# Another order of the work in each step of three narrow cross attentions

## The chip, the cores and the metric

The kernel is one program on 1 core of a Trainium2 chip. The metric is the device time of one execution in microseconds (us); the median of three executions of the kernel before is 3112.84 us.

## What is computed

Four layers of a perceiver: each adds a cross attention to `x` (32 samples, 64 queries, width 256), then a mixing stage, then a feed-forward stage. The change touches the cross attentions of layers 1, 2 and 3. They have one formula, cut here to what matters:

```
q = ln(x @ Wq + bq)                      16 heads of 16, normed per head
k = ln(y_main @ Wk + bk)                 112 context rows of a sample
v = y_main @ Wv + bv
k_dca, v_dca = the same from y_dca       the other 16 context rows
ctx = attn(q, k, v) + attn(q, k_dca, v_dca)
x = x + ctx @ Wo + bo
```

The two softmaxes of a head, over 112 and over 16 context rows, are separate, so each has its own maximum and its own sum.

## The kernel before

The function `cross_attention_narrow` (called three times, for L1, L2 and L3) writes one program for each engine by hand, with semaphores between them. Its main part is a loop over steps `n`, from -1 to 34. In a step the samples stand at different places of a pipeline:

- **score** (L1540, TensorE): the scores of sample n+1 into the buffer `p_s`. There is one such buffer, so it waits for `shifted`, sample n's subtraction on VectorE.
- **maximum** (L1772), **subtraction** (L1782), **row sums** (L1790) and **reciprocal** (L1793) on VectorE; the sums are those of sample n-1. ScalarE's **exponential** (L1701) is sample n's. GpSimd multiplies with the reciprocals (L1856, semaphore `normed`) and then spreads the queries of sample n+2 (L1849, `q_spread`, for which that sample's score waits).
- **values** (L1551, TensorE): sample n-2, into the bank `p_v`; ScalarE's two **value copies** (L1710, L1712, `v_copied`) move it to `vx`.
- **turn** (L1561, TensorE): 8 transposes of sample n-2's probabilities into `p_t`; ScalarE's two **probability copies** (L1728, `turned_read`) move them out.
- **mix** (L1574, TensorE): probabilities by values of sample n-3; ScalarE's **u copy** (L1718, `mixed_read`) moves the result out.
- **output product** (L1581, TensorE), in even steps from 4 on, for two samples; VectorE's **x addition** (L1798, `added`), in odd steps from 5 on, reads it. The mix two samples on waits for that addition, because both use the bank `p_y`.

Beside this nine **units** (three of queries, six of keys, 512 columns each) are normed for later samples. A unit takes three steps, and from step 4 on the kinds of step repeat by threes:

- **kind A** (steps 4, 7, ... 22): TensorE's **unit product** (L1499 for queries, L1503 for keys) into `p_t`, ScalarE's **bias** (L1652, `biased`) and **squares** (L1667, `squared`). The turn of this step waits for the bias, because it uses the same `p_t`.
- **kind B** (steps 5, 8, ... 23): TensorE's **tally** (L1517), which adds the squares up in the bank `p_v`, and ScalarE's **inverse** (L1684 and L1687 or L1691).
- **kind C** (steps 6, 9, ... 24): TensorE's **widening** (L1527) into `p_t`, VectorE's **unit multiplication** (L1766, `scaled`), for which this step's turn waits. GpSimd's addition L1841 follows.
- steps 25 to 34 have no unit; from step 31 on there is no score either.

The order of the work is written out in the `step` function of each engine, and every engine takes its instructions in that order. TensorE's order before, in one step:

```
score(n+1); unit product or widening; values(n-2); mix(n-3);
tally, after a wait for v_copied of values(n-2);
turn(n-2), in kinds A and C after biased or scaled; output product
```

ScalarE's: exponential, bias, value copies, u copy, inverse, probability copies, squares. VectorE's: maximum, unit multiplication, subtraction, row sums, reciprocal, x addition.

Of the kernel before, what the change touches and what calls it, by code (L numbers as in the profile page):

```python
# [1341 lines left out]
def cross_attention_narrow(k, layer):  # L1342
# [9 lines left out]
    with ExitStack() as ctx:  # L1352
# [83 lines left out]
        def within(n, lo, hi):  # L1436
            return lo <= n < hi
# [14 lines left out]
        def _(pe):  # L1452
# [91 lines left out]
            def values(n):  # L1544
                if n >= 1:
                    pe.wait_ge(sem["v_copied"], n)
                else:
                    pe.wait_ge(ln.sem["rstd"], 1)
                    pe.wait_ge(s_o, 32)
                pe.wait_ge(sem["logged"], tallied_before(n + 2))  # L1550
                pe.matmul(p_v[:, :], k.ctxT[:, ts(n, S2)], wv[:, :, :].rearrange("p n f -> p (n f)"), start=True, stop=True, skip_group_check=True).then_inc(sem["valued"], 1)  # L1551

            def turn(n):
# [30 lines left out]
            def step(n):  # L1584
                if -1 <= n < B - 1:
                    score(n + 1)
                units = at_step(n)
                for i, part in units:
                    if part == 0:
                        turned_before(n)  # L1590
                        project(i)
                    elif part == 2:
                        turned_before(n)
                        widen(i)
                if within(n, 2, B + 2):
                    values(n - 2)
                if within(n, 3, B + 3):
                    mix(n - 3)
                for i, part in units:
                    if part == 1:  # L1600
                        if n >= 2:
                            pe.wait_ge(sem["v_copied"], n - 1)
                        else:
                            pe.wait_ge(ln.sem["rstd"], 1)
                        tally(i)
                if within(n, 2, B + 2):
                    for i, part in units:
                        if part == 0:
                            pe.wait_ge(sem["biased"], i + 1)
                        elif part == 2:  # L1610
                            pe.wait_ge(sem["scaled"], i + 1)
                    turn(n - 2)
                if n >= 4 and n % 2 == 0:
                    project_out((n - 4) // 2)

            ln.means(pe)
            keep_warm(pe, k, p_tw[:, 0, :], 1)
# [27 lines left out]
        def _(act):  # L1645
# [48 lines left out]
            def own(n, rows):  # L1694
                return vx[rows, n % 2, :, :, :].rearrange("p o (r j) (s d) -> p (o r) (j s) d", j=2, s=2)[:, :, 0:4:3, :]

            def step(n):
                units = at_step(n)
                if within(n, 0, B):
                    act.wait_ge(sem["shifted"], n + 1)  # L1700
                    act.activation(prob[:, n % 4, :, :, :], prob[:, n % 4, :, :, :], ACT.Exp, scale=0.25).then_inc(sem["exped"], 1)  # L1701
                for i, part in units:
                    if part == 0:
                        add_bias(i)
                if within(n, 2, B + 2):
                    m = n - 2
                    act.wait_ge(sem["valued"], m + 1)
                    if m >= 2:
                        act.wait_ge(sem["mixed"], m - 1)
                    act.copy(own(m, slice(0, P)), p_v[:, 0:D].rearrange("p (g j d) -> p g j d", j=2, d=HD)).then_inc(sem["v_main"], 1)  # L1710
                    act.wait_ge(sem["v_main"], m + 1)
                    act.copy(own(m, slice(0, DCA)), p_v[0:DCA, D:2 * D].rearrange("p (g j d) -> p g j d", j=2, d=HD)).then_inc(sem["v_copied"], 1)  # L1712
                if within(n, 3, B + 3):
                    m = n - 3
                    act.wait_ge(sem["mixed"], m + 1)
                    if m >= 4:
                        act.wait_ge(sem["out_proj"], m // 2 - 1)
                    act.copy(us[:, m // 2 % 2, :, ts(m % 2, S)], p_o).then_inc(sem["mixed_read"], 1)  # L1718
                for i, part in units:
                    if part == 1:  # L1720
                        inverse(i)
                if within(n, 2, B + 2):
                    m = n - 2
                    for o in range(H2):
                        act.wait_ge(sem["turned"], 2 * m + o + 1)
                        if m >= 1:
                            act.wait_ge(sem["mixed"], m)
                        act.copy(probT[:, o, :, :, :].rearrange("p r j t -> p (r j t)"), p_t[:, o, :, :].rearrange("p r q -> p (r q)")).then_inc(sem["turned_read"], 1)  # L1728
                for i, part in units:
                    if part == 0:  # L1730
                        squares(i)
# [28 lines left out]
        @block.vector  # L1760
        def _(v):
            def multiply(i):
                kind, c = UNITS[i]
                dst = q if kind == QN else kk
                v.wait_ge(sem["widened"], i + 1)
                v.tensor_tensor(dst[:, :, ts(c, CH)], biased[:, i % 2, :, :], front(i)[:, :, :], ALU.mult).then_inc(sem["scaled"], 1)  # L1766

            def step(n):
                if within(n, 0, B):
                    v.wait_ge(sem["scored"], n + 1)  # L1770
                    for m, (s0, s1) in enumerate(SEG):
                        mx = v.tensor_reduce(nmax[:, n % 2, m, :, :], p_s[:, :, :, s0:s1], AX, ALU.max, negate=True)  # L1772
                    mx.then_inc(sem["maxed"], 1)
                for i, part in at_step(n - 1):
                    if part == 2:
                        multiply(i)
                if within(n, 0, B):
                    v.wait_ge(sem["maxed"], n + 1)
                    if n >= 4:
                        v.wait_ge(sem["turned"], 2 * n - 6)  # L1780
                    for m, (s0, s1) in enumerate(SEG):
                        sub = v.tensor_tensor(prob[:, n % 4, :, :, s0:s1], p_s[:, :, :, s0:s1], bcast(nmax[:, n % 2, m, :, :], 3, s1 - s0), ALU.add)  # L1782
                    sub.then_inc(sem["shifted"], 1)
                if n < H2:
                    out_bias_of(n)
                if within(n, 1, B + 1):
                    m = n - 1
                    v.wait_ge(sem["exped"], n)
                    for seg, (s0, s1) in enumerate(SEG):
                        total = v.tensor_reduce(rsum[:, 0, m % 4, seg, :, :], prob[:, m % 4, :, :, s0:s1], AX, ALU.add)  # L1790
                    total.then_inc(sem["summed"], 1)
                    v.wait_ge(sem["summed"], n)
                    v.reciprocal(rsum[:, 1, m % 4, :, :, :], rsum[:, 0, m % 4, :, :, :]).then_inc(sem["recip"], 1)  # L1793
                if n >= 5 and n % 2 == 1:
                    t = (n - 5) // 2
                    v.wait_ge(sem["out_proj"], t + 1)
                    v.wait_ge(sem["biased_x"], 2)
                    v.tensor_tensor(k.x[:, :, ts(t, P)], k.x[:, :, ts(t, P)], p_y, ALU.add).then_inc(sem["added"], 1)  # L1798

            def add_bias(i):  # L1800
                kind, c = UNITS[i]
                v.wait_ge(sem["projected"], i + 1)
                v.wait_ge(sem["copied"], 2)
                for o in range(H2):
                    to, of = (ap.rearrange("p (b s) -> p b s", s=S2) for ap in (biased[:, i % 2, o, :], front(i)[:, o, :]))
                    for (m, to), (_, of) in zip(columns(kind, to), columns(kind, of)):
                        j = v.tensor_scalar(to, of, bc[:, m, o:o + 1], None, ALU.add)
                j.then_inc(sem["biased"], 1)

            def out_bias_of(o):  # L1810
                v.wait_ge(sem["out_bias"], 2)
                v.wait_ge(ln.sem["centred"], NCH)
                v.tensor_scalar(k.x[:, o, :], k.x[:, o, :], out_bias[:, 1, o:o + 1], None, ALU.add).then_inc(sem["biased_x"], 1)

            for c in range(NCH):
                ln.centre(v, c)
            add_bias(0)
            ln.scale(v, 0)
            ln.scale(v, 1)
            multiply(0)  # L1820
            ln.scale(v, 2)
            ln.scale(v, 3)
            multiply(1)
            multiply(2)
            for n in range(B + 4):
                step(n)
# [1835 lines left out]
```

## Time and profile before

| | |
|---|---|
| median of 3 executions (3112.57 to 3114.63) | 3112.84 us |
| span of the profiled execution | 3107.8 us |
| median less that span (what lies around the span) | 5.0 us |
| instructions in the span | 49980 |
| TensorE matmul busy | 2746.9 us, 88% |
| VectorE busy | 1863.8 us, 60% |
| ScalarE busy | 1414.8 us, 45% |
| GpSimd busy | 993.6 us, 32% |

The own time of the profiled execution is its span and what lies around it; the runs list times without naming the profiled one, so the median stands for it. Most of the span belongs to stages that the change does not touch. The main loops of the three stages lie at about 905 to 1089, 1587 to 1771 and 2107 to 2290 us of the span. A busy TensorE is not one at its peak, since matmuls overlap and their ends are modelled; distances between the starts of groups say more. A number in square brackets behind an instruction is the time that its engine sat idle before it, with what ended that time.

### The profile page before, as it was taken

The page shows a single profiled execution, that of the slowest core. Times are in us where ns is not written, and L with a number is a line of the kernel's source. Part 1 is how long each engine was busy: PE and PEld are TensorE (multiplying, and loading weights), DVE is VectorE, ACT ScalarE, POOL GpSimd, SP SyncE. Part 2 cuts the span into 40 slices and gives each one's busy share as a digit, 9 for nine tenths or more (in the row PEclk, how much of TensorE's full clock was granted, in tenths as well). Part 3 has the DMA queues.
Part 4 walks back from the last instruction along what each step waited for, and adds up shares of the span by engine and source line. Part 5 has one row for each costly group of instructions (what it writes and reads, how often), then busy time and mean ns, then how long its engine had stood idle before and what let it go on. Part 6 is the DMA issues. An engine that isn't in the chain of part 4 may idle for free. (4 is left out here: it accounts for less than half of the span.)

```text
span 3107.8 us, 49980 instructions
## 1 busy us (share of the span) xinstructions
PE 2746.9 (88%) x18724; PEld 1708.9 (55%) x18724; DVE 1863.8 (60%) x2492; ACT 1414.8 (46%) x2714; POOL 993.6 (32%) x836
## 2 busy tenths in 40 slices
PE   8999997999989988899989875668989798999899
PEld 5989863466556647433346532225644455554687
DVE  3555546322258737444468678767865799996433
ACT  4333345122147646322257554445767666653123
POOL 0111100133225512000035400005520799992462
PEclk9999998999999999999999988889999999999999
DMA  4000003311110000200000000000000212113124
GB/s 159 1 0 0 0 7 112 114 47 46 55 50 2 2 22 2 85 1 0 2 21 2 15 0 0 0 22 2 2 30 18 77 69 80 68 58 112 57 87 150
DMA packets 73446, 122.61 MB, mean 39 GB/s; under 512 B 11616, under 2 KB 54240, under 8 KB 72736
## 3 DMA queue, kind: packets, MB, share of 16 engines
q1 hardware_dynamic: 64320, 95.48, 9.2%
q0 software_dynamic: 8928, 24.39, 2.5%
q8 instruction: 137, 2.24, 0.3%
q14 instruction: 61, 0.50, 0.1%
HBM read 101.10 MB, written 18.74 MB: 39 GB/s over the span
## 5 line engine op out<-in xcount | busy, mean ns | idle before, releaser
L3398 POOL TENSOR_TENSOR h<-ssm_u,ss_bc 128x1024 f32<-128x1024 f32 x88 | 205.6, 2354 | 0.0
L3361 ACT ACTIVATE ssm_p_h<-ss_delta,ss_decay 128x256 f32<-128x256 f32 x352 | 146.6, 463 | 123.9 <-DVE ctxT L3435 82.9
L3308 PE MATMUL ssm_p_y<-ctxT,ident 128*128 128x512 f32 x412 | 187.8, 596 | 0.0
L650 POOL TENSOR_TENSOR xw_prob<-xw_prob,xw_rsum 128x512 f32<-128x512 f32 x64 | 65.8, 1039 | 355.2 <-DVE xw_rsum L631 355.2
L3430 DVE TENSOR_TENSOR_SCAN ssm_p_h<-ssm_p_h,h 128x1024 f32<-128x1024 f32 x64 | 145.8, 2279 | 8.7 <-ACT ssm_p_h L3361 6.8
L3388 POOL TENSOR_TENSOR ctxT<-ctxT,ss_bc 128x1024 f32<-128x1024 f32 x50 | 117.4, 2355 | 19.3 <-DVE ctxT L3428 19.3
L500 PEld LDWEIGHTS xw_p_q<-h,xw_m_h 128*128 128x128 f32 x1024 | 116.8, 192 | 8.9 <-issue 8.9
L509 PEld LDWEIGHTS xw_p_q<-xw_u,xw_vo_h 128*128 128x128 f32 x1024 | 115.8, 192 | 10.7 <-ACT xw_u L580 10.2
L3308 PEld LDWEIGHTS ssm_p_y<-ctxT,ident 128*128 128x128 f32 x412 | 76.6, 192 | 79.5 <-issue 78.3
L509 PE MATMUL xw_p_q<-xw_u,xw_vo_h 128*128 128x128 f32 x1024 | 118.2, 276 | 0.0
L500 PE MATMUL xw_p_q<-h,xw_m_h 128*128 (+1 forms) x1024 | 117.0, 275 | 1.3 <-PEq L60 1.3
L3292 PE MATMUL ssm_p_h<-ssm_b_diagonal,ssm_uT 128*128 128x128 f32 x640 | 82.9, 284 | 39.9 <-DVE ctxT L3435 19.5
L2432 ACT ACTIVATE lmm_hidden<-lmm_p_h,vecs 128x512 f32<-128x512 f32 x64 | 43.5, 687 | 156.0 <-PE lmm_p_h L2392 108.1
L3292 PEld LDWEIGHTS ssm_p_h<-ssm_b_diagonal,ssm_uT 128*128 128x128 f32 x640 | 77.7, 197 | 63.8 <-issue 55.2
L1196 DVE TENSOR_TENSOR L0f_hidden<-L0f_silu,L0b_p_u 128x512 f32<-128x512 f32 x39 | 26.8, 688 | 125.2 <-PE L0b_p_u L1131 125.2
L621 DVE TENSOR_TENSOR xw_prob<-xw_p_s,xw_mask_bias 128x512 f32<-128x512 f32 x64 | 44.0, 687 | 91.7 <-PE xw_p_s L518 91.7
L2461 DVE TENSOR_TENSOR lmm_hidden<-lmm_hidden,lm_weights 128x512 f32<-128x512 f32 x64 | 44.1, 689 | 89.5 <-ACT lmm_hidden L2432 89.5
L1830 POOL MEMSET L3x_vx<- 128x1024 f32 x1 | 1.0, 952 | 302.2 <-POOLq L60 302.2
L1856 POOL TENSOR_TENSOR L1x_prob<-L1x_prob,L1x_rsum 128x896 f32<-128x896 f32 x64 | 65.3, 1042 | 73.5 <-DVE L1x_rsum L1793 73.5
L1856 POOL TENSOR_TENSOR L2x_prob<-L2x_prob,L2x_rsum 128x896 f32<-128x896 f32 x64 | 65.3, 1042 | 73.5 <-DVE L2x_rsum L1793 73.5
L1856 POOL TENSOR_TENSOR L3x_prob<-L3x_prob,L3x_rsum 128x896 f32<-128x896 f32 x64 | 65.3, 1042 | 72.3 <-DVE L3x_rsum L1793 72.3
L1105 POOL DMA_INDIRECT L0f_rows_out<-L0b_y,L0f_row_of x39 | 38.5, 986 | 146.7 <-DVE L0b_y L1204 146.7
(865 smaller groups left out, 7146.6 us busy)
## 6 DMA issues: line engine op xcount, KB each, us to landing
ss_bc<-ss_bc_rows SPq DMA_DIRECT2D x24, 896.0 KB, 4.3
ss_bc<-ss_bc_rows SPq DMA_DIRECT2D x8, 768.0 KB, 4.1
L3f_rows<-L3f_rows_out SPq DMA_DIRECT2D x16, 384.0 KB, 4.0
L0f_wg<-in_L_ffn_gate SPq DMA_DIRECT2D x9, 512.0 KB, 9.9
L0f_wu<-in_L_ffn_up SPq DMA_DIRECT2D x9, 512.0 KB, 9.8
L0f_wd<-in_L_ffn_down SPq DMA_DIRECT2D x9, 512.0 KB, 9.7
L0f_rows<-L0f_rows_out SPq DMA_DIRECT2D x16, 256.0 KB, 4.1
x<-in_xT SPq DMA_DIRECT2D x1, 2048.0 KB, 7.5
```

Of the source, the lines that this page charges most:

```text
L500: mm = pe.matmul(p_q5[:, q % 2, h % 4 // 2, :, h % 2, :], m_h[:, h, a, :], k.h[:, a, ts(i, P)], start=h % 4 == 0 and a == 0, stop=a == H2 ...
L509: mm = pe.matmul(p_q[:, 0, ts(o, P)], vo_h[:, h, ts(o, P)], us[:, h, :], start=h == 0 and o == 0, stop=h == NH - 1, skip_group_check=True)
L621: v.tensor_tensor(prob[:, part, :], p_s[:, part, :], bcast(bias[:, ts(n, S2)], 1, 4), ALU.add).then_inc(sem["masked_scores"], 1)
L650: g.tensor_tensor(prob[:, part, :], prob[:, part, :], bcast(rsum[:, 1, part], 2, S2), ALU.mult).then_inc(sem["normed"], 1)
L1856: scaled = g.tensor_tensor(prob[:, m % 4, :, :, s0:s1], prob[:, m % 4, :, :, s0:s1], bcast(rsum[:, 1, m % 4, seg, :, :], 3, s1 - s0), ALU. ...
L2461: v.tensor_tensor(hh[:, m % 2, j, :], hh[:, m % 2, j, :], wb[:, j, ts(c, CH)], ALU.mult).then_inc(sem["weighed"], 1)
L3292: mm = pe.matmul(p_h[:, n % 2, e * CT + b * P:e * CT + b * P + P], uT[:, c % 2, b, ts(e, P)], db[:, i, b, :], start=True, stop=True, skip_ ...
L3308: mm = pe.matmul(p_y[:, 2 * half:2 * half + 2, :].rearrange("p e t -> p (e t)"), k.ident[:, :], weighed[n % RING_W][:, ts(half, CH)], star ...
L3361: i = act.activation(out[:, ts(e, CT)], delta[:, e, ts(c, CT)], ACT.Exp, scale=decay[:, E4 * s + e:E4 * s + e + 1])
L3388: g.tensor_tensor(tiles(weighed[n % RING_W]), tiles(weighed[n % RING_W]), bcast(bcs[:, row_c(s), :], 1, E4), ALU.mult).then_inc(sem["weigh ...
L3398: g.tensor_tensor(tiles(drive[n % RING]), u[:, c % 2, :, :], bcast(bcs[:, row_b(s), :], 1, E4), ALU.mult).then_inc(sem["driven_g"], 1)
L3430: v.tensor_tensor_scan(slot, factor, term, 0.0, ALU.mult, ALU.add).then_inc(sem["scanned"], 1)
```

## The change

In a step TensorE now mixes right after the score; the tally comes next and waits for `v_copied` of one sample less; the output product comes ahead of the turn; and in kind B the values come last, behind the turn. ScalarE's u copy comes right after the exponential, and in kind B its probability copies come ahead of the value copies. VectorE's x addition comes ahead of the row sums. No instruction is added or removed.

```diff
-                pe.wait_ge(sem["logged"], tallied_before(n + 2))
+                pe.wait_ge(sem["logged"], tallied_before(n + 3))
...
             def step(n):
                 if -1 <= n < B - 1:
                     score(n + 1)
+                if within(n, 3, B + 3):
+                    mix(n - 3)
                 units = at_step(n)
+                tallies = any(part == 1 for _, part in units)
                 for i, part in units:
                     if part == 0:
                         turned_before(n)
                         project(i)
-                    elif part == 2:
-                        turned_before(n)
-                        widen(i)
-                if within(n, 2, B + 2):
-                    values(n - 2)
-                if within(n, 3, B + 3):
-                    mix(n - 3)
-                for i, part in units:
-                    if part == 1:
-                        if n >= 2:
-                            pe.wait_ge(sem["v_copied"], n - 1)
+                    elif part == 1:
+                        if n >= 3:
+                            pe.wait_ge(sem["v_copied"], n - 2)
                         else:
                             pe.wait_ge(ln.sem["rstd"], 1)
                         tally(i)
+                    else:
+                        turned_before(n)
+                        widen(i)
+                if within(n, 2, B + 2) and not tallies:
+                    values(n - 2)
+                if n >= 4 and n % 2 == 0:
+                    project_out((n - 4) // 2)
                 if within(n, 2, B + 2):
...
                     turn(n - 2)
-                if n >= 4 and n % 2 == 0:
-                    project_out((n - 4) // 2)
+                    if tallies:
+                        values(n - 2)
```

On ScalarE, the step after the change (`spread_values` holds the two value copies, `turned` the two probability copies, word for word as before):

```diff
                     act.activation(prob[:, n % 4, :, :, :], prob[:, n % 4, :, :, :], ACT.Exp, scale=0.25).then_inc(sem["exped"], 1)
-                for i, part in units:
-                    if part == 0:
-                        add_bias(i)
-                if within(n, 2, B + 2):
...
                 if within(n, 3, B + 3):
                     m = n - 3
                     act.wait_ge(sem["mixed"], m + 1)
...
                 for i, part in units:
-                    if part == 1:
+                    if part == 0:
+                        add_bias(i)
+                    elif part == 1:
                         inverse(i)
                 if within(n, 2, B + 2):
...
+                    if tallies:
+                        turned(n - 2)
+                        spread_values(n - 2)
+                    else:
+                        spread_values(n - 2)
+                        turned(n - 2)
                 for i, part in units:
                     if part == 0:
                         squares(i)
```

On VectorE the block of the x addition moves, unchanged, from behind the reciprocal to just behind the subtraction:

```diff
                     sub.then_inc(sem["shifted"], 1)
+                if n >= 5 and n % 2 == 1:
+                    t = (n - 5) // 2
+                    v.wait_ge(sem["out_proj"], t + 1)
+                    v.wait_ge(sem["biased_x"], 2)
+                    v.tensor_tensor(k.x[:, :, ts(t, P)], k.x[:, :, ts(t, P)], p_y, ALU.add).then_inc(sem["added"], 1)
                 if n < H2:
                     out_bias_of(n)
```

## Rows read from the trace of the kernel before

**Rows 1.** The three stages' windows summed, busy us by engine.
```profile
sum 551.00, PE 490.98 PEld 333.28 DVE 437.89 ACT 362.62 POOL 304.98; mean PE 163.66 PEld 111.09 DVE 145.96 ACT 120.87 POOL 101.66
```

**Rows 2.** Waits of TensorE in the first stage: us in total, times, longest.
```profile
PE L1x_p_v L1517 <- ACT L1x_vx L1712: 6.7, 8, 2.6
```

**Rows 3.** Timeline, steps 9 and 10: start us, us, engine, line, operation [idle before].
```profile
961.98 0.73 PE L1540 MATMUL L1x_p_s<-L1x_k,L1x_qx 32*128 32x128 f32 x16
...
963.98 1.21 DVE L1766 TENSOR_TENSOR L1x_q<-L1x_biased,L1x_p_t 128x1024 f32<-128x1024 f32 x1
...
966.54 0.73 PE L1540 MATMUL L1x_p_s<-L1x_k,L1x_qx 32*128 32x128 f32 x16
...
967.20 2.16 PE L1503 MATMUL L1x_p_t<-ctxT,L1x_wkc 128*128 128x448 f32 x8
...
969.19 1.08 PE L1551 MATMUL L1x_p_v<-L1x_wv,ctxT 128*128 128x512 f32 x2
969.39 1.57 ACT L1652 ACTIVATE L1x_biased<-L1x_p_t,L1x_bc 128x448 f32<-128x448 f32 x4 [1.30 <-PE L1x_p_t L1503]
...
970.20 0.65 PE L1574 MATMUL L1x_p_y<-L1x_probT,L1x_vx 128*32 128x64 f32 x32
...
971.01 1.09 PE L1561 MATMUL L1x_p_t<-ident,L1x_prob 128*128 128x128 f32 x8 [0.16 <-ACT L1x_biased L1652]
...
971.94 1.06 PE L1581 MATMUL L1x_p_y<-L1x_u,L1x_wo 128*128 128x128 f32 x8
...
972.93 0.73 PE L1540 MATMUL L1x_p_s<-L1x_k,L1x_qx 32*128 32x128 f32 x16
973.04 0.42 DVE L1798 TENSOR_TENSOR x<-x,L1x_p_y 128x256 f32<-128x256 f32 x1 [1.24 <-PE L1x_p_y L1581]
```

**Rows 4.** Timeline, steps 11 and 12.
```profile
975.57 0.65 PE L1517 MATMUL L1x_p_v<-L1x_square,L1x_tally 128*32 128x128 f32 x16 [0.27 <-ACT L1x_vx L1712]
...
977.17 0.73 PE L1540 MATMUL L1x_p_s<-L1x_k,L1x_qx 32*128 32x128 f32 x16
977.18 1.05 ACT L1728 COPY L1x_probT<-L1x_p_t 128x512 f32<-128x512 f32 x2
...
978.28 1.16 PE L1527 MATMUL L1x_p_t<-L1x_rv,L1x_heads 64*128 64x128 f32 x16 [0.39 <-ACT L1x_probT L1728]
...
979.49 1.22 DVE L1766 TENSOR_TENSOR L1x_k<-L1x_biased,L1x_p_t 128x1024 f32<-128x1024 f32 x1 [0.24 <-PE L1x_p_t L1527]
...
982.93 0.73 PE L1540 MATMUL L1x_p_s<-L1x_k,L1x_qx 32*128 32x128 f32 x16
```

**Rows 5.** Timeline, end of step 13, and step 14.
```profile
987.41 1.09 PE L1561 MATMUL L1x_p_t<-ident,L1x_prob 128*128 128x128 f32 x8 [0.16 <-ACT L1x_biased L1652]
...
988.43 0.73 PE L1540 MATMUL L1x_p_s<-L1x_k,L1x_qx 32*128 32x128 f32 x16
989.06 1.07 ACT L1667 ACTIVATE L1x_square<-L1x_biased 128x1024 f32<-128x1024 f32 x1
...
990.96 0.37 ACT L1710 COPY L1x_vx<-L1x_p_v 128x256 f32<-128x256 f32 x1
...
991.63 0.25 ACT L1718 COPY L1x_u<-L1x_p_y 128x128 f32<-128x128 f32 x1
...
991.78 0.64 PE L1517 MATMUL L1x_p_v<-L1x_square,L1x_tally 128*32 128x128 f32 x16 [0.98 <-ACT L1x_vx L1712]
...
994.27 0.73 PE L1540 MATMUL L1x_p_s<-L1x_k,L1x_qx 32*128 32x128 f32 x16
```

**Rows 6.** Timeline, scores that open steps 24 and 26.
```profile
1042.72 0.73 PE L1540 MATMUL L1x_p_s<-L1x_k,L1x_qx 32*128 32x128 f32 x16
...
1053.67 0.73 PE L1540 MATMUL L1x_p_s<-L1x_k,L1x_qx 32*128 32x128 f32 x16 [1.80 <-POOL L1x_qx L1849]
```

**Rows 7.** Timeline, the last steps: transposes of samples 29 and 31.
```profile
1077.58 1.09 PE L1561 MATMUL L1x_p_t<-ident,L1x_prob 128*128 128x128 f32 x8
...
1083.41 1.09 PE L1561 MATMUL L1x_p_t<-ident,L1x_prob 128*128 128x128 f32 x8
```

More of the change, by code:

```diff
@@ L1695, in own, with spread_values, turned @@
                 return vx[rows, n % 2, :, :, :].rearrange("p o (r j) (s d) -> p (o r) (j s) d", j=2, s=2)[:, :, 0:4:3, :]
+            def spread_values(m):
+                act.wait_ge(sem["valued"], m + 1)
+                if m >= 2:
+                    act.wait_ge(sem["mixed"], m - 1)
+                act.copy(own(m, slice(0, P)), p_v[:, 0:D].rearrange("p (g j d) -> p g j d", j=2, d=HD)).then_inc(sem["v_main"], 1)
+                act.wait_ge(sem["v_main"], m + 1)
+                act.copy(own(m, slice(0, DCA)), p_v[0:DCA, D:2 * D].rearrange("p (g j d) -> p g j d", j=2, d=HD)).then_inc(sem["v_copied"], 1)
+            def turned(m):
+                for o in range(H2):
+                    act.wait_ge(sem["turned"], 2 * m + o + 1)
+                    if m >= 1:
+                        act.wait_ge(sem["mixed"], m)
+                    act.copy(probT[:, o, :, :, :].rearrange("p r j t -> p (r j t)"), p_t[:, o, :, :].rearrange("p r q -> p (r q)")).then_inc(sem["turned_read"], 1)
             def step(n):
                 units = at_step(n)
+                tallies = any(part == 1 for _, part in units)
                 if within(n, 0, B):
@@ L1701, in step @@
                     act.activation(prob[:, n % 4, :, :, :], prob[:, n % 4, :, :, :], ACT.Exp, scale=0.25).then_inc(sem["exped"], 1)
-                for i, part in units:
-                    if part == 0:
-                        add_bias(i)
-                if within(n, 2, B + 2):
[L1706 to L1712, printed above, removed]
                 if within(n, 3, B + 3):
@@ L1719, in step @@
                 for i, part in units:
-                    if part == 1:
+                    if part == 0:
+                        add_bias(i)
+                    elif part == 1:
                         inverse(i)
                 if within(n, 2, B + 2):
[L1723 to L1728, printed above, removed]
+                    if tallies:
[4 more added lines that the diff above has]
+                        turned(n - 2)
                 for i, part in units:
@@ L1793, in step @@
                     v.reciprocal(rsum[:, 1, m % 4, :, :, :], rsum[:, 0, m % 4, :, :, :]).then_inc(sem["recip"], 1)
[L1794 to L1798, printed above, removed]
             def add_bias(i):
```

## The prediction

> **What bounds the kernel now.** I read the windows first. In the three stages' main loops TensorE's matmuls are busy for 491 of 551 us, VectorE for 438, ScalarE for 363 and GpSimd for 305 [rows 1]. TensorE is the engine to fill, and at most 60 us of it are idle. The list of waits comes second: the one that repeats is the tally's, eight times in a stage, 6.7 us together and 2.6 us at most, put down to the value copies [rows 2]. That is what the change goes for. The timeline comes third, because an average doesn't say which chain ends each kind of step. I measure a step from score to score.
>
> Before, an odd C step takes 4.56 us (961.98 to 966.54) and an even A step 6.39 (to 972.93) [rows 3]. The odd B step takes 4.24 (972.93 to 977.17), the even C step 5.76 (to 982.93) and the odd A step 5.50 (to 988.43), the even B step 5.84 (to 994.27) [rows 3 to 5]: 32.29 us for six steps. The odd C step is no TensorE chain: its next score comes 2.56 us after the start of the unit multiplication [rows 3], as multiplication and subtraction on VectorE stand between. Odd and even differ by the output product.
>
> **Lengths**, from start to start: score 0.66, unit product 1.99, values 1.01 (1.05 with a full load time), turn 0.93, output product 0.99 [rows 3]; turn to score 1.02 [rows 5]; tally and turn 1.60, so tally 0.58 [rows 4]. Widening to next score is 4.65 [rows 4], which leaves 0.6 for the mix. VectorE reads the output product 0.11 after its last issue (1.10 less 0.99) [rows 3]. The bias starts 2.19 after the unit product and takes 1.57; TensorE goes on 0.05 after it [rows 3].
>
> **No work is added or removed**, so all of the cost is in waits. I lay out each kind of step, with times from its own score.
>
> *Kind A, odd.* The mix now stands ahead of the unit product, which starts at 0.66 + 0.60 = 1.26. Only the values are left between the product and the turn: TensorE would be there at 4.26. The bias ends at 1.26 + 2.19 + 1.57 = 5.02, so the turn starts at 5.07 and the step takes 6.09. Before, it took 5.50, with a wait of 0.16 [rows 5]. Cost 0.6. The mix used to cover the bias.
>
> *Kind A, even.* The output product, now ahead of the turn, covers the bias: 4.26 + 0.99 + 1.02 = 6.27 against 6.39, a gain of 0.1. VectorE's x addition, now ahead of the row sums, waits for this product until 5.4; the next maximum is only 0.2 behind its score for that, and the next product gives it back. Nothing is taken for it.
>
> *Kind B.* The wait for the value copies goes: they are a step old. What is late next is the squares. Behind the turn of kind A come probability copies and then squares, which start 1.65 and end 2.72 after the turn (987.41, 989.06 and its 1.07) [rows 5]. The score follows the turn by 1.02, so the squares end at 1.70 and the tally starts at 1.75, where TensorE would be at 1.26. A wait of 0.5 takes the place of 0.27 in the odd and 0.98 in the even step [rows 4, 5]. Odd: tally 2.33, turn 3.26, values to 4.3, against 4.24: cost 0.1. Even: the output product needs the u copy. On ScalarE squares and exponential take 1.90 together (989.06 to 990.96) [rows 5], so the exponential ends near 2.5 and the u copy of 0.25 [rows 5] at 2.8. Product to 3.8, turn to 4.75, values to 5.8, against 5.84: nothing.
>
> *Kind C.* Its mix stands right behind the score and needs the value copies of the step before, whose values now came last. After an even B step they end 5.8 + 0.1 + 0.8 = 6.7, that is 0.9 into the C step (0.8 is the copies' 990.96 to the tally's 991.78 [rows 5]). Then mix to 1.5, and the multiplication starts 1.21 after the widening [rows 4] at 2.7. The next score is 2.56 later, at 5.3, against 4.56. Cost 0.7, of which 0.45 would be there without any wait, since the mix alone pushes the widening. After an odd B step ScalarE is late: u copy to 2.7, the inverse, probability copies from 3.6 (1.61 behind the tally, and a quarter more for the u copy now ahead), 1.05 long [rows 4], value copies to 5.4: 1.1 into the even C step. There the mix runs to 1.7 and the rest, 4.65 less the mix, to 5.75, against 5.76: nothing, as a wait of 0.39 at the widening goes [rows 4].
>
> Steps 7 to 23 hold three odd and three even A, three odd and three even B, three odd and two even C steps: 1.8 - 0.3 + 0.3 + 0 + 2.1 + 0 = 3.9 us.
>
> *Steps 24 and 25* took 10.95 us, the end of it a wait of 1.80 for GpSimd's query spread [rows 6]. GpSimd's chain starts at VectorE's reciprocal. The multiplication ahead of that starts 2.9 into the step instead of 2.32 (977.17 to 979.49) [rows 4], and the x addition, 0.42 long [rows 3], moves ahead of it, for about 0.3. Cost 0.9.
>
> *Steps 26 to 30* are VectorE's, whose work is the same. *The end:* from step 31 no score stands between turn and mix. The mix is through about 2.1 after the turn (the probability copies end near 1.75, by the squares' start at 1.65 [rows 5], and half a mix follows); values and, in the even step, the output product follow ahead of the next turn: 3.1 + 4.1 = 7.2 between the turns of samples 29 and 31, against 5.83 [rows 7]. The earlier x addition spares what step 31's mix now loses. Cost 1.4. *The start:* in step 2 the tally still waits for squares, so of its 2.6 us [rows 2] I take 0.65 as gained, and 0.25 of it lost again in step 3: -0.4, between 0 and -2.6.
>
> **Sum:** 3.9 + 0.9 + 1.4 - 0.4 = 5.8 us for a stage, 17.4 for three. The profiled execution has a span of 3107.8, which becomes 3125.2; with the 5.0 us around it, by which the median of 3112.84 stands above it, that is 3130 us. The terms that no row shows in their new place are those of kinds B and C. If no cost arises there but the mix's push on the widening (0.45), a stage pays 1.8 - 0.3 + 1.4 + 0.9 + 1.4 - 2.6 = 2.6: 3121. If the even B and C steps lose 0.4 each besides, five times, it is 7.8: 3136.
>
> The Trainium skill (Perfetto Trace Analysis, Optimization Strategy) says that the same gap repeating on the engine that should be full can mean too few buffers in SBUF or PSUM. The trace agrees so far that the tally and the values share the bank `p_v`, and the wait comes back eight times [rows 2]. [...]
>
> **Rivals.**
> 1. *Faster: the tally's wait goes and nothing takes its place.* 6.7 us in each stage [rows 2], 20 in three: 3093. For it: the wait is real, and TensorE is the fullest engine. Against: the squares end 2.7 after the turn [rows 5], half a microsecond after TensorE gets to the tally. It decides if they end within 2.2. With half of it, 3103.
> 2. *No change: single buffers hold the work.* Each of `p_v`, `p_t`, `p_s` and `p_y` has one copy, so the 6.7 us of wait [rows 2] move to another user at the same length: 3113. The Trainium skill's page named above speaks for it. Against: the odd A and C steps get longer without any such bank becoming free earlier.
> 3. *Slower still: GpSimd is late in every round of six steps,* not in step 24 alone. Its spread of queries after an even C step ends about 11.8 after that step's score, where TensorE wants it at 5.75 + 6.09 = 11.84. If it ends 0.5 later, three more waits in a stage, and their echo on ScalarE: 4 to 8 us in all, 3134 to 3138. For it: 1.80 of wait already [rows 6].
>
> **How the numbers follow.** About 0.2% (6 us) is what a measurement of this kernel can tell from no change. My forecast, slower by 17 us, has a chance of 0.58, as it is a chain of short waits of which each could be misread but all large ones point one way. Rival 3 has 0.10, rival 2 0.14, rival 1 0.18. So faster 0.18, same 0.14, slower 0.68. The range goes from 3104, which takes in rival 2 and the half of rival 1, to 3140, over rival 3. The likeliest case alone has 3119 to 3137.
>
> **What would show it.** In the profile after: odd A steps of 6.1 us and odd C steps of 5.3; the tally waiting 0.5 us for squares; mixes in C steps waiting for value copies; the turn of odd A steps waiting 0.8 for the bias; 11.8 us for steps 24 and 25; 7.2 us between the last turns. I am wrong if odd A and C steps keep their length, or if the tally starts within 1.3 us of the score.

## The result, and the profile after

The changed kernel takes 3131.35 us (median of 4 runs, 3126.78 to 3135.16), the kernel before beside it 3112.70. The ratio is 1.0052, with a 95% interval from 1.0041 to 1.0064: slower by 0.5%. Run again on another chip it gave 1.0066 (1.0053 to 1.0080). The forecast was 3130, slower by 17; measured are 18.6. By spans it is more than by medians. In every execution that lists both, the time is 1.8 us above its span, so of the 5.0 us that the part ahead of the prediction calls "around the span" some 3.2 come from a profiled execution that was faster than the median; the changed kernel's profiled one, 3132.71 us, is 1.4 slower than its median.

The profiled execution has a span of 3130.9 us, 23.1 more than before. I measure each stage's main loop from its first score to the end of its last x addition. Before, the three loops take 182.19, 182.19 and 180.95 us; after, 189.19, 188.11 and 189.09. That is 21.1 of the 23.1. The rest lies outside the loops, where the profiled executions of all kernels here take between 2554.9 and 2564.5 us. Split by steps, from the distances between scores (us):

| | before, stages 1, 2, 3 | after, stages 1, 2, 3 | forecast for a stage | measured, mean |
|---|---|---|---|---|
| steps -1 to 6 | 43.9, 43.9, 44.2 | 45.9, 44.8, 45.8 | -0.4 | +1.5 |
| steps 7 to 23 | 93.3, 93.3, 93.3 | 96.0, 96.0, 96.0 | +3.9 | +2.7 |
| steps 24, 25 | 10.95, 10.96, 10.96 | 11.75, 11.75, 11.75 | +0.9 | +0.8 |
| steps 26 to 29 | 17.5, 17.5, 16.0 | 17.7, 17.7, 17.6 | 0 | +0.6 |
| last score to the end | 16.46, 16.46, 16.46 | 17.86, 17.86, 17.85 | +1.4 | +1.4 |
| sum | | | +5.8 | +7.0 |

In steps 26 to 29 what differs is one step and the clock. Step 26 takes 5.77, 5.77 and 4.21 us in the three stages before, and 5.72, 5.63 and 5.72 after. Where it is long, TensorE's granted clock over it is 0.70, which means that for a part of it the lower of the two levels (1.2 GHz) was granted and for the rest the full 2.4 GHz; where it is short, it is 1.00. Just before it TensorE waits for GpSimd's spread, 1.80 us before and 3.02 after. Around step 26 of the kernel before, in the first stage and in the third (window, its length, TensorE busy, granted clock, DMA share, GB/s):

```profile
1050.00:1061.00 11.00, 9.20 (x125) 0.84 0.01 1
2252.00:2263.00 11.00, 9.19 (x159) 1.00 0.02 4
```

The length of step 26 is 5.6 to 5.8 us or 4.1 to 4.2 in the runs below too, in one stage or another of kernels of either order. So a sum of loops can be 1.6 us off for each stage. Steps 4 to 24 run at a granted clock of 1.00 in every trace, and "steps 7 to 23" is the safer measure of an order.

The waits of TensorE after, first stage (us in total, times, longest). The value copies of [rows 2] are gone as a releaser of the tally. The tally now waits for squares, which the list calls "issue" (in the timelines below a tally starts 0.2 us after the squares end):

```profile
PE L1x_p_v L1517 <- issue: 7.8, 9, 2.0
PE L1x_p_s L1540 <- POOL L1x_qx L1858: 4.4, 3, 3.0
...
PE L1x_p_t L1561 <- ACT L1x_biased L1654: 2.0, 3, 0.7
PE L1x_p_y L1574 <- ACT L1x_probT L1712: 1.8, 4, 0.6
PE L1x_p_y L1574 <- ACT L1x_vx L1705: 1.6, 7, 0.3
```

The timeline after, an even A step (10) and the odd B step (11) behind it. It answers to [rows 3, 4]:

```profile
965.93 0.73 PE L1540 MATMUL L1x_p_s<-L1x_k,L1x_qx 32*128 32x128 f32 x16 [0.19 <-DVE L1x_prob L1791]
...
969.17 1.08 PE L1551 MATMUL L1x_p_v<-L1x_wv,ctxT 128*128 128x512 f32 x2
...
970.09 1.05 PE L1581 MATMUL L1x_p_y<-L1x_u,L1x_wo 128*128 128x128 f32 x8
...
970.99 1.09 PE L1561 MATMUL L1x_p_t<-ident,L1x_prob 128*128 128x128 f32 x8
...
972.02 0.73 PE L1540 MATMUL L1x_p_s<-L1x_k,L1x_qx 32*128 32x128 f32 x16
972.64 1.07 ACT L1669 ACTIVATE L1x_square<-L1x_biased 128x1024 f32<-128x1024 f32 x1
...
973.93 0.65 PE L1517 MATMUL L1x_p_v<-L1x_square,L1x_tally 128*32 128x128 f32 x16 [0.60 <-issue]
...
976.39 0.73 PE L1540 MATMUL L1x_p_s<-L1x_k,L1x_qx 32*128 32x128 f32 x16
```

Step 10 takes 6.09 us (965.93 to 972.02), against 6.39 before. No bias wait stands at the turn, since the output product covers it. Values to output product are 0.92 and output product to turn 0.90. Step 11 takes 4.37: its tally comes 1.91 after the score, after 0.60 of idle time, when the squares are done (972.64 and 1.07).

The odd A step 13, which answers to the end of step 13 in [rows 5]:

```profile
981.87 0.73 PE L1540 MATMUL L1x_p_s<-L1x_k,L1x_qx 32*128 32x128 f32 x16
...
985.11 1.08 PE L1551 MATMUL L1x_p_v<-L1x_wv,ctxT 128*128 128x512 f32 x2
985.31 1.57 ACT L1654 ACTIVATE L1x_biased<-L1x_p_t,L1x_bc 128x448 f32<-128x448 f32 x4 [1.59 <-PE L1x_p_t L1503]
...
986.93 1.09 PE L1561 MATMUL L1x_p_t<-ident,L1x_prob 128*128 128x128 f32 x8 [0.74 <-ACT L1x_biased L1654]
...
987.47 0.61 POOL L1858 TENSOR_TENSOR L1x_qx<-L1x_q,half_of 128x256 f32<-128x256 f32 x1
...
988.13 0.73 PE L1540 MATMUL L1x_p_s<-L1x_k,L1x_qx 32*128 32x128 f32 x16
```

The turn waits 0.74 for the bias, where it waited 0.16. The score comes 1.20 after the turn, not 1.02: GpSimd's query spread ends only at 988.08. The step takes 6.26 us, 5.50 before.

The odd C step 15, which answers to the first rows of [rows 3]:

```profile
993.63 0.73 PE L1540 MATMUL L1x_p_s<-L1x_k,L1x_qx 32*128 32x128 f32 x16
...
994.14 0.36 ACT L1705 COPY L1x_vx<-L1x_p_v 16x256 f32<-16x256 f32 x1
...
994.55 0.66 PE L1574 MATMUL L1x_p_y<-L1x_probT,L1x_vx 128*32 128x64 f32 x32 [0.20 <-ACT L1x_vx L1705]
...
996.35 1.22 DVE L1775 TENSOR_TENSOR L1x_k<-L1x_biased,L1x_p_t 128x1024 f32<-128x1024 f32 x1 [0.64 <-PE L1x_p_t L1527]
...
998.91 0.73 PE L1540 MATMUL L1x_p_s<-L1x_k,L1x_qx 32*128 32x128 f32 x16 [0.20 <-DVE L1x_prob L1791]
```

The mix waits 0.20 for the value copies (994.14 and 0.36), and the widening comes only behind it. The multiplication starts 2.72 after the score, and 2.56 later comes the next score: 5.28 us for 4.56.

The end of the stage, which answers to [rows 7]:

```profile
1079.27 1.04 PE L1561 MATMUL L1x_p_t<-ident,L1x_prob 128*128 128x128 f32 x8
...
1080.86 0.81 PE L1574 MATMUL L1x_p_y<-L1x_probT,L1x_vx 128*32 128x64 f32 x32 [0.55 <-ACT L1x_probT L1712]
...
1083.46 1.04 PE L1561 MATMUL L1x_p_t<-ident,L1x_prob 128*128 128x128 f32 x8
...
1086.55 1.04 PE L1561 MATMUL L1x_p_t<-ident,L1x_prob 128*128 128x128 f32 x8
```

From the turn of sample 29 to that of sample 31 it is now 7.28 us, 5.83 before, and each mix waits for probability copies with TensorE idle.

### The profile page after: what moved, and what is told of

Read it like the earlier page. It is cut to its first block and busy times, and to the rows that moved or that the text cites. A ratio compares the mean times of both kernels' runs of the same rounds, so it can differ in the third digit from the quotient of the medians.

```text
span 3130.9 us, 49976 instructions
## 1 busy us (share of the span) xinstructions
PE 2747.9 (88%) x18720; PEld 1720.0 (55%) x18724; DVE 1861.9 (59%) x2492; ACT 1415.8 (45%) x2714; POOL 994.1 (32%) x836
## 5 line engine op out<-in xcount | busy, mean ns | idle before, releaser
L621 DVE TENSOR_TENSOR xw_prob<-xw_p_s,xw_mask_bias 128x512 f32<-128x512 f32 x64 | 43.9, 687 | 91.7 <-PE xw_p_s L518 91.7
```

The costliest lines, as they stand in the source:

```text
L621: v.tensor_tensor(prob[:, part, :], p_s[:, part, :], bcast(bias[:, ts(n, S2)], 1, 4), ALU.add).then_inc(sem["masked_scores"], 1)
```

## The experiments

Expected times are on the scale of the first comparison, with 3112.7 us for the kernel before. Beside the experiments it took about 3105, so they are to be compared by the ratio: 3119 us, for one, is 1.0020.

The theory to test: the cost is a sum of short waits that the mix's early place makes in odd steps, plus the end of the stage. The rivals: VectorE's x addition ahead of the row sums; single buffers, by which a wait only moves; and, as the table shows a start that the forecast missed, TensorE's clock. All kernels compute the same. "Loops" is the sum of the three main loops in the profile, against 545.3 us before; "ratio" is to the kernel before on the same chip.

**First group.** Four runs beside 13 of the kernel before (median 3105.04 us).

```diff
 # e1: x addition behind the reciprocal again
-                if n >= 5 and n % 2 == 1:      (behind sub.then_inc)
+                if n >= 5 and n % 2 == 1:      (behind v.reciprocal)
```

> The changed kernel with VectorE's x addition back behind the reciprocal; all else as changed. Theory (short waits from the mix's new place, no cost from the x addition): slower still. The mix now stands early in odd steps and waits for that addition, which in an odd A step would end about 1.8 us after the score instead of before it: odd A steps 1.0 us longer, three in a stage, steps 27 and 29 a few tenths; GpSimd gets 0.3 back in step 24. Some 3 to 4 us a stage, 3138 to 3146 us in all. Rival (the x addition ahead of the row sums holds up the reciprocals and so GpSimd): faster than the changed kernel, 3115 to 3122 us.

Measured: 3132.5 us, ratio 1.0091 (1.0076 to 1.0107), loops 571.3. In the first stage step 13 takes 7.15 us (6.26 in the changed kernel), steps 7 and 19 8.40 and 7.15 (7.32 and 6.12). Steps 7 to 23 take 99.3 to 99.4 us a stage (96.0), and the last score to the end 18.9 (17.9). The loops show less, because here step 26 was short in all three stages and step 1 of the first took 6.99 us (8.93). The timeline of the experiment at step 13:

```profile
980.98 0.73 PE L1543 MATMUL L1x_p_s<-L1x_k,L1x_qx 32*128 32x128 f32 x16
...
982.08 0.36 DVE L1873 TENSOR_TENSOR x<-x,L1x_p_y 128x256 f32<-128x256 f32 x1
...
982.70 0.65 PE L1577 MATMUL L1x_p_y<-L1x_probT,L1x_vx 128*32 128x64 f32 x32 [1.00 <-DVE x L1873]
```

The mix waits for the x addition and is 1.72 behind its score. The ratio is as the theory had it (3138 to 3146 us, 1.0081 to 1.0107), only the few tenths in steps 27 and 29 came at the end of the stage instead. So the early x addition is no cost here: it is what makes the early mix possible. Step 25 gets 0.33 back (5.93 for 6.26), the reciprocal being earlier for GpSimd. The rival falls.

```diff
 # e2 to e4, e7, e8: a step for which old(n) holds runs the order of before
 # (TensorE and ScalarE; in e2 to e4 the x addition stays early)
+            def step(n):
+                if old(n):
+                    return step_as_before(n)
 # e2
+            return n >= 7 and n % 2 == 1 and any(part != 1 for _, part in at_step(n))
 # e3
+            return n >= 5 and any(part == 1 for _, part in at_step(n))
 # e4
+            return n >= 25
```

> The changed kernel with the order of before on TensorE and ScalarE in the odd steps of kinds A and C alone (steps 7, 9, 13, 15, 19, 21). Theory: the mix ahead of unit product and widening is what costs in odd steps; A goes from 6.26 back to 5.5 us and C from 5.28 to 4.56. By the traces of before and after that is 4.1 us a stage, 12 in all: 3119 us (3115 to 3123). Rival (single buffers, the wait only moves): the steps around get longer by as much, 3128 to 3134 us.

Measured: 3113.98 us, ratio 1.0026 (1.0016 to 1.0036), loops 554.6, 11.8 less than the changed kernel. Of these, 10.4 lie in steps 7 to 23 (92.5 to 92.6 us a stage for 96.0) and 1.5 in one short step 26. So the order gives back 3.5 us a stage, where the theory had 4.1, and not in every step that it named. The odd C steps are 4.56 again. Step 13 stays at 6.26, and instead the B step behind it goes from 5.50 to 5.05, as its squares begin with the score (989.29 us for both) and not 0.46 behind it. The timeline shows why:

```profile
984.30 0.25 DVE L1873 RECIPROCAL L1x_rsum<-L1x_rsum 128x16 f32<-128x16 f32 x1
...
984.63 2.04 POOL L1931 TENSOR_TENSOR L1x_prob<-L1x_prob,L1x_rsum 128x896 f32<-128x896 f32 x2 [3.77 <-DVE L1x_rsum L1873]
...
986.63 2.04 POOL L1916 TENSOR_TENSOR L1x_k<-L1x_k,vecs 128x896 f32<-128x896 f32 x2
...
987.64 1.09 PE L1564 MATMUL L1x_p_t<-ident,L1x_prob 128*128 128x128 f32 x8 [0.16 <-ACT L1x_biased L1691]
...
988.62 0.61 POOL L1924 TENSOR_TENSOR L1x_qx<-L1x_q,half_of 128x256 f32<-128x256 f32 x1
...
989.29 0.73 PE L1543 MATMUL L1x_p_s<-L1x_k,L1x_qx 32*128 32x128 f32 x16 [0.55 <-POOL L1x_qx L1924]
```

The turn is early (0.16 of bias wait again), but the score waits 0.55 for GpSimd's spread, at the end of a chain from the reciprocal: 0.33, 2.0, 2.0 and 0.61 us. That is the mechanism of the third rival of the prediction. It sits in two of the three odd A steps (in step 19 the wait is 0.41, in step 7 there is none), and the bias wait hid most of it.

> The changed kernel with the order of before in the steps of kind B from 5 on (values and mix ahead of the tally, output product behind the turn, value copies first). Theory: kind B itself is near even, its odd steps gain 0.1 and its even ones lose 0.2, and the C steps behind it get 0.3 back, as the mix there no longer waits for value copies: about -0.7 us a stage, 3129 us (3126 to 3132). Rival (the tally's new wait for the squares, 0.5 us seven times in a stage, is the main cost): 3 us a stage, 3122 us.

Measured: 3132.12 us, ratio 1.0085 (1.0072 to 1.0099), loops 574.1. Both expectations have the wrong sign: steps 7 to 23 get 2.9 us longer a stage (98.9), not shorter. The odd B step 11 takes 4.95 us:

```profile
975.55 0.73 PE L1543 MATMUL L1x_p_s<-L1x_k,L1x_qx 32*128 32x128 f32 x16
976.18 1.07 ACT L1706 ACTIVATE L1x_square<-L1x_biased 128x1024 f32<-128x1024 f32 x1
...
978.09 0.37 ACT L1740 COPY L1x_vx<-L1x_p_v 128x256 f32<-128x256 f32 x1
...
978.90 0.64 PE L1520 MATMUL L1x_p_v<-L1x_square,L1x_tally 128*32 128x128 f32 x16 [0.98 <-ACT L1x_vx L1742]
...
980.50 0.73 PE L1543 MATMUL L1x_p_s<-L1x_k,L1x_qx 32*128 32x128 f32 x16
```

Behind a new even A step ScalarE is late. Its squares begin 0.63 after the score (in the kernel before they began at 972.67, 0.26 ahead of the score of [rows 3]), exponential and value copies follow, and a tally that waits for those copies starts 3.35 after its score, 1.44 later than with the new order. The odd C steps lengthen too, 5.62 for 5.28. So the new kind B is a gain once the new kind A stands before it. I had priced it against the B steps of the kernel before.

> The changed kernel with the order of before in steps 25 to 34 alone. Theory: in the last four steps the mix waits for the probability copies with nothing before it, 1.4 us in each stage; steps 25 to 30 are bound by VectorE and GpSimd and stay: 3127 us (3125 to 3130), and 5.83 us between the turns of samples 29 and 31 instead of 7.28. Rival (the end of a stage is set by the last x addition alone, which waits for GpSimd): 3131 us.

Measured: 3123.76 us, ratio 1.0059 (1.0045 to 1.0073), loops 565.1. The last score to the end is 16.01 (17.86), but steps 27 and 29 take 4.75 us each (3.7 to 3.9 and 4.1 to 4.2). Together nothing is gained: steps 26 to the end take 35.5 us in both. From the turn of sample 29 to that of sample 31 it is 6.09 us, not the 5.83 expected. The timeline at step 27:

```profile
1061.91 0.73 PE L1543 MATMUL L1x_p_s<-L1x_k,L1x_qx 32*128 32x128 f32 x16
1062.02 0.42 DVE L1863 TENSOR_TENSOR x<-x,L1x_p_y 128x256 f32<-128x256 f32 x1 [2.02 <-PE L1x_p_y L1584]
1062.36 1.27 DVE L1870 TENSOR_REDUCE L1x_rsum<-L1x_prob 128x8 f32<-128x896 f32 x2
...
1066.67 0.73 PE L1543 MATMUL L1x_p_s<-L1x_k,L1x_qx 32*128 32x128 f32 x16 [1.37 <-POOL L1x_qx L1924]
```

With the output product behind the turn, the early x addition starts late, the row sums behind it, and the chain through GpSimd holds the next score. Here the early x addition does cost: two places of the change, x addition and output product, belong together. e8 below, with both as before from step 24 on, has 16.46 at the end without the longer steps 27 and 29.

**Second group.** Four runs beside 24 of the kernel before (3104.82 us).

```diff
 # e5 and e6: matmuls of 512 columns into p_v, before the waits in steps 0, 1 and 2
+                    keep_warm(pe, k, p_v[:, :], 3)      (tally of units 3 and 4)
+                        keep_warm(pe, k, p_v[:, :], 5)  (product of unit 4)
 # e6 also: old(n) is True, x addition behind the reciprocal
```

> The changed kernel with filler matmuls (3, 5 and 3 of 512 columns into the bank p_v) in the idle times of TensorE in steps 0, 1 and 2, where it waits for squares and for the first query multiplication. Theory: the order itself makes step 2 shorter (5.4 us, as one stage of the run with the ends as before showed, against 6.0 before); the 7.1 to 7.7 us in the profile of the changed kernel are the granted clock of 0.50 in that stretch. So step 1 goes from 8.9 to about 7.0 and step 2 to 5.4: 3.5 to 4.3 us a stage, 12 in all against the changed kernel, ratio to before near 1.001. Rival (the order makes step 2 long, the clock is only its companion): step 2 stays above 7 us, ratio 1.005.

> The order of before in every step, with the same filler matmuls. Theory: step 1 goes from 8.7 to about 7.0, step 2 stays at 6.0, as it waits for the value copies at either clock: 1.7 us a stage, ratio to before 0.998. Rival (the clock costs nothing there, the waits end at the same time): 1.000.

Measured: e5 3122.79 us, ratio 1.0052 (1.0039 to 1.0065), loops 561.6; e6 3115.73, ratio 1.0031 (1.0019 to 1.0043), loops 554.1. In e5 step 2 falls from 7.6 to 5.89 at a granted clock of 1.00, so the most of its excess was the clock's, but step 1 is 8.42. In e6 step 1 is 8.42 and step 2 8.8 to 10.5. A filler takes 0.95 us, twice what I had reckoned, so the fillers overran the idle times and were a cost of their own. As a measure of what the clock costs both are inconclusive; f2 and f3 measure it again.

```diff
 # e7, with the x addition behind the reciprocal
+            return n >= 31 or n >= 3 and n % 2 == 1 and any(part != 1 for _, part in at_step(n))
 # e8, with the x addition behind the reciprocal
+            return n >= 24 or not (n % 2 == 0 and any(part == 0 for _, part in at_step(n)) or any(part == 1 for _, part in at_step(n)))
```

> Order of before in odd steps of kinds A and C and from step 31 on, x addition back behind the reciprocal, all else as changed. Theory: the run with odd A and C as before left step 13 at 6.26 us because its score waited 0.55 us for GpSimd's query spread, whose chain begins at the reciprocal of the even C step before. With the x addition behind the reciprocal that chain is 0.3 shorter: step 13 at 5.9, steps 7 to 23 at 91.7 us against 92.6 there and 93.3 before. End of the stage as before (16.5). Ratio to before 0.998 to 1.002. Rival (the bias, not GpSimd, holds step 13): it stays at 6.26.

Measured: 3105.96 us, ratio 1.0000 (0.9990 to 1.0010), loops 543.1. Step 13 is at 5.93, so GpSimd's chain holds it there. But step 14 gives that back (5.39 for 5.05), and steps 7 to 23 stay at 92.6 to 92.7, not 91.7. The loops would not be below those of the kernel before if step 26 had not been short in all three stages.

> The new order only in kind B (steps 0 to 23) and in even A steps; kind C, odd A, steps from 24 on and the x addition as before. Theory: these two kinds are the ones where the new order gains (even A 6.09 for 6.39, even B 5.5 for 5.8), and the even C step as before gives GpSimd its time back, so that odd A is 5.5: six steps in 31.6 us against 32.3, steps 7 to 23 some 1.6 us shorter than before, 0.9 lost in steps 2 and 3 to the clock, ratio to before 0.998 to 1.000. Rival (the gains of new B depend on the new order around it): six steps in 32.3 us or more.

Measured: 3099.55 us, ratio 0.9985 (0.9976 to 0.9995), loops 542.4. In the first stage steps 9 to 14 take 4.56, 6.08, 4.37, 5.31, 5.50 and 5.67: 31.49 us for 32.29. Steps 7 to 23 take 91.8 to 92.0, against 93.3 before. By time this version is 0.15% ahead of the kernel before; that is less than the 0.2% which the prediction took as what can be told, but its interval leaves out 1, and the steps show the gain directly.

**Third group.** Four runs beside 18 of the kernel before (3105.35 us). The fillers are now 2, 3 and 2.

```diff
 # f2 (on the changed kernel), f3 (on the order of before, none in step 2), f4 (on e8)
-                    keep_warm(pe, k, p_v[:, :], 3)
+                    if i == EARLY or not old(2):
+                        keep_warm(pe, k, p_v[:, :], 2)
-                        keep_warm(pe, k, p_v[:, :], 5)
+                        keep_warm(pe, k, p_v[:, :], 3)
```

> The changed kernel itself, as the measure for the other runs on the same chip. If the ratio to before is a property of the order, it is again 1.005 to 1.006. If it was a matter of one chip or of where the clock fell in other stages, it differs from 1.0052 by more than 0.002.

Measured: 3126.17 us, ratio 1.0066 (1.0053 to 1.0080), loops 566.4, the same as in the first profile. The steps repeat to about 0.01 us, apart from those in which the granted clock changes.

> The changed kernel with 2, 3 and 2 filler matmuls in steps 0, 1 and 2. A filler took 0.95 us in the earlier run, not the 0.43 reckoned with, so 3, 5 and 3 ran past the idle times; these fit into them. Theory (order and clock are two things): step 1 at 7.0 us, step 2 at 5.4 to 5.5, 3.5 to 4 us a stage less than the changed kernel, ratio 1.001 to 1.002. Rival (a clock that drops elsewhere instead): the loop gets shorter and the ratio stays at 1.005.

Measured: 3111.56 us, ratio 1.0024 (1.0013 to 1.0034), loops 552.3, 14 less than f1. Steps -1 to 6, where the fillers are, account for 12.3 of it (41.35 us a stage for 44.8 to 45.8); the rest is step 26, short in two stages and longer in the third. Steps 1 and 2 take 6.93 and 5.28 us (8.93 and 7.59). The stretch in windows (columns as above; 0.50 is the lower level, 1.2 GHz), first the changed kernel, then f2:

```profile
915.00:920.00 5.00, 4.77 (x24) 0.50 0.00 0
920.00:925.00 5.00, 3.40 (x25) 0.50 0.00 0
925.00:930.00 5.00, 5.00 (x68) 0.77 0.01 3
```

```profile
915.00:920.00 5.00, 4.75 (x22) 1.00 0.00 0
920.00:925.00 5.00, 4.82 (x46) 1.00 0.00 0
925.00:930.00 5.00, 4.47 (x75) 1.00 0.01 3
```

> The order of before with 2 and 3 fillers in steps 0 and 1 and none in step 2. Step 1 at 7.0 us instead of 8.7, step 2 at 6.0 as before, 1.7 us a stage: ratio 0.998. If the clock drops in step 2 instead, step 2 gets longer than 6.0 and the ratio is 1.000.

Measured: 3104.12 us, ratio 0.9994 (0.9985 to 1.0003), loops 542.9. Step 1 is 6.94, but step 2 takes 6.9 to 7.3 for 6.0:

```profile
918.82 0.73 PE L1551 MATMUL L1x_p_s<-L1x_k,L1x_qx 32*128 32x128 f32 x16
...
923.23 1.08 PE L1528 MATMUL L1x_p_v<-L1x_square,L1x_tally 128*32 128x128 f32 x16 [2.63 <-ACT L1x_vx L1750]
...
924.24 1.97 PE L1572 MATMUL L1x_p_t<-ident,L1x_prob 128*128 128x128 f32 x8
...
926.14 0.74 PE L1551 MATMUL L1x_p_s<-L1x_k,L1x_qx 32*128 32x128 f32 x16
```

From the turn to the next score it is 1.90 us, where it is 1.02 in [rows 5], behind the 2.63 us in which the tally waits for value copies. The granted clock over step 2 is 0.77, 0.87 and 0.75 in the three stages. Most of the gain of step 1 is given back by a clock that falls in step 2: the second of the two expected outcomes. The wait alone doesn't decide it: the same 2.63 us stand in step 2 of the kernel before, which had a granted clock of 1.00 there in two stages.

> The kernel with the new order in kind B and in even A steps alone (it gave 0.9985), with 2, 3 and 2 fillers. If both gains add up: steps 7 to 23 at 91.9 us, step 1 at 7.0 and step 2 at 5.4, some 3.5 us a stage less than without fillers, ratio 0.995 to 0.996, the fastest of all. If the clock drops elsewhere, 0.998.

Measured: 3091.79 us, ratio 0.9951 (0.9938 to 0.9965), loops 530.5, each stage 176.8 or 176.9. It is the fastest of all, 0.5% ahead of the kernel before; both gains add up. Step 26 is still long in all three stages.

The loops account for most of the times. Against the kernel before, loops and medians differ by +26.0 and +27.5 us (e1), +9.2 and +8.9 (e2), +28.8 and +27.1 (e3), +7.0 and +6.2 (f2), -14.8 and -13.6 (f4). They agree least in e7 (-2.2 and +1.1) and e8 (-3.0 and -5.3), whose profiled executions were 3.6 us faster and 5.2 slower than the median.

## Why the prediction was right, and where its terms were off

**Right, and shown.** Odd A steps: 0.6 forecast, and 0.57, 0.76 and 0.62 measured in steps 7, 13 and 19; the bias wait of step 13 is 0.74. In e8, with these steps and the even C steps as before, step 13 is back at 5.50. Odd C steps: 0.7 and 0.72, with the multiplication at 2.72 after the score where the sum had 2.7; e2 brings them back to 4.56. Kind B: the squares take the place of the value copies at the tally, 1.91 after the score where the sum had 1.75. Steps 24 and 25: 0.9 and 0.8, and e1 shows 0.33 of it to be the x addition's, as assumed (0.3). The end: 1.4 and 1.4; 7.2 us between the turns were forecast and 7.28 came. These waits are what the theory named. The signs by which the forecast called itself wrong, odd A and C steps of the old length or a tally within 1.3 us of the score, did not come.

**Terms mis-sized, in favour of the change.** Even steps were costed at -0.1 (A), 0 (B) and 0 (C). They gain 0.30 (step 10), 0.34 (step 14) and 0.28 (step 12). I had taken one length for each group of matmuls whatever stands behind it: values 1.01 to 1.05, output product 0.99. In even A and C steps, with output product behind values and turn behind output product, it is 0.92 and 0.90. That is some 0.2 less for each, and the trace before could have warned of it: there, from step 30 on, the output product took 0.89 ahead of values. In the even B step 14 the u copy ends 2.63 after the score, not 2.8, and turn and values take 0.88 and 0.95. That is why steps 7 to 23 lose 2.7, not 3.9. No run varies the group lengths alone; they are read from the traces.

**The start is the term that failed.** The step read: "in step 2 the tally still waits for squares, so of its 2.6 us I take 0.65 as gained", -0.4 in all. At full clock it holds: 5.28 us for step 2 in f2 and f4, against 6.0 before, though step 3 loses 0.46 (5.35 for 4.89), not 0.25. But in the changed kernel the clock granted over step 2 is 0.50, 0.75 and 0.50 in the three stages, and it takes 7.1 to 7.7 us. Of the 24 stages here with the new order in step 2 and no fillers, 23 take 7.05 to 7.8 us, with 0.50 to 0.76 granted, and one (in e4) 5.43, with 0.87; the kernel before took 6.01 in all three. Why the order brings the clock down there no run shows. No term for the clock stood in the sum, nor a rival, though it differed between the stages already before, in steps 1, 2 and 26. f2 prices it: fillers take 12.3 us off the start of the changed kernel's loops. Not all of that is what the change brought: step 1 was slow before as well (8.67, 8.68 and 8.93 us, 6.94 in f3).

**So the nearness of the number is in part luck.** An estimate of the order alone, all at full clock: the first stage of f2 takes 183.2 us, and the kernel before would take 179.0 with f3's step 1 and with steps 26 to 29 of its own third stage. That is 4.2 us a stage, where 5.8 were forecast. The other 2.8 of the 7.0 are the clock's, in steps 1 to 3 and 26, for which the sum had nothing. The order was priced 1.6 too dear and the clock 2.8 too cheap. The medians, 18.6 us apart, also lie nearer to the forecast than the loops do with 21.1; beside f1 they are 20.8 apart.

**GpSimd** (third rival, 0.10) was given as a margin that might be missed. It is missed by 0.18 us in step 13 and by 0.03 in step 19, and in e2 by 0.55 and 0.41, but not in step 7. So it is true beside the forecast, and small, not in its place. The bias and GpSimd don't add up in an odd A step. With GpSimd's wait alone (e2) step 13 takes 6.26 and step 19 6.12; with the bias alone it would be 6.08, an estimate from the turn at 5.06 and the usual 1.02 to the score.

**The faster rival** would have needed the squares within 2.2 us of the turn; they end 2.7 after it. **No change** by single buffers (the Trainium skill, Perfetto Trace Analysis, Optimization Strategy) isn't borne out. The page says that such a gap can mean too few buffers, not that an order can't help: e8 keeps every buffer and takes 0.8 us from a round of six steps. What the rival had right is that the wait at the tally moved rather than vanished: in the first stage it waits 8.7 us before (6.7 of it for value copies) and 7.8 after.

Open is what decides whether the clock falls in step 26. Step 26 was long in two stages of three before, in all three after and in f4, in one of e3 and in none of e1 and e7; in the third stage of f2 it took 6.87 us, with 0.56 granted. It wasn't tried to keep TensorE busy ahead of it, where it waits for GpSimd.

## What to carry to other kernels

Read each kind of step by the chain that ends it: one order gained up to 0.3 us in even steps and lost 0.6 to 0.8 in odd steps of kinds A and C, and choosing the order by kind and parity turned +0.5% into -0.15%. Before trusting a sum of such tenths, look at the granted clock stage by stage: here its share was 2.8 us a stage beside 4.2 of the order. Before moving work away from a wait, ask what that work covered and which result is late next. A piece of a change may be worth something only beside another piece, so test it in the new surroundings, not the old.

## What was not expected of the hardware

The granted clock decides as much as the order in the first steps: with TensorE waiting three times for about 2 us (1.99, 2.17 and 1.83), it fell to 0.50 in steps 1 and 2 (8.93 and 7.69 us in the first stage), and with 7 fillers of 0.95 us it stayed at 1.00 (6.93 and 5.28). Five such fillers ahead of one wait of 2.63 us (f3) gave little, as the clock fell there instead. A 512-column f32 filler took 0.95 us of TensorE at a granted clock of 1.00. The length of a group of matmuls went with what followed it: values 1.01 to 1.05 us ahead of a mix, 0.92 ahead of an output product.
